# Decoder kernel on one core: couplings on ScalarE, a shorter choice of the expert, first norm in place, queries one turn earlier

## The chip, the core and the metric

The kernel runs on one core of a Trainium2 chip. The core has five engines that run their own instruction streams and meet only at semaphores: TensorE (PE), VectorE (DVE), ScalarE (ACT), GpSimd (POOL) and SyncE (SP), which issues the DMAs. The metric is the device time of one launch in microseconds; smaller is better.

## What is computed

Two decoder layers over x (32 sequences of 256 rows, 256 wide) and a context (32 sequences of 120 rows), with a layer norm behind each of six sublayers:

```python
x = _layernorm(x + _L0_attn_ref(x))          # random features: exp(x P - |x|^2/2) times a fixed matrix
x = _layernorm(x + _L0_xattn_ref(x, ctx))    # cross attention, 16 heads of 16
x = _layernorm(x + _L0_ffn_ref(x))           # 3 cycles of a coupling network, below
x = _layernorm(x + _L1_attn_ref(x))          # Mamba: convolution, gates, scan over 512 channels x 16 states
x = _layernorm(x + _L1_xattn_ref(x, ctx))    # gated unit whose weights are the context
x = _layernorm(x + _L1_ffn_ref(x))           # 8 experts, the one with the highest probability counts
```

The third sublayer computes, three times over, four small layers with gelu and a sigmoid (the "gate"), mixes them with a global gate of the sequence into a coupling, and rotates the state with it: `out = out + coupling * _twist(out)`. The sixth takes `gate = max(softmax(logits))` and `idx = argmax(softmax(logits))` of each row.

## The kernel before

Two sequences (512 rows) make a group, and there are 16 groups. The work on a group is cut into three parts: **f** (sublayers 1 to 3), **m** (the Mamba) and **b** (sublayers 4 to 6 behind the Mamba). A **turn** does f of one group, m of the group before, b of the one before that, and the first steps of the group to come (**nxt**): its random features, keys, values, first projection and first norm. There are 18 turns; f, m and nxt meet in 14 of them (turns 1 to 14, counted from 0), the last two have no f.

Nothing schedules this: on each engine the function `turn` or `turn_` writes the order out by hand, and semaphores tie the engines together. What matters here, with the lines of the program printed below:

- On DVE the spine is `states`, 64 scans (L1087, one for each of 4 channel blocks and 16 states) with 4 output steps (L1093) between, and everything else is put between two of them. A scan reads a decay that ACT has computed into a ring of 12 (`decays`, L1479), and a PSUM bank with the square of the convolved input of its channel block (L1474). ACT computes that square inside `decays`, ahead of decay number `SQUARE_AT[c]`, and not before the last scan of the block in front. The first scan of the last block is number 48; its square stands ahead of decay 59. POOL adds the scanned states up (L1671).
- `norm_add`, `norm_stats` on DVE, `norm_rstd` on ACT (Ln and Exp, L398 and L400), `norm_apply` on DVE (L405), `norm_turn` on PE (8 transposes, L413) and `norm_copy` on ACT (L419) make one layer norm. n1 to n6 are the six norms; `ln1_sum` and `ln3_sum` are the sums and statistics of n1 and n3.
- `cycle` on PE and ACT is one of the three cycles, for both sequences in turn; ACT ends it with the gate (L1430), and `rotate` on DVE computes the coupling (L1038) and the rotation (L1040 to L1043).
- `route` and `pick_expert` on DVE choose the expert, `combine` (L1199) adds the experts' outputs by `experts` on PE (through two banks).
- `mamba_out` on PE brings the residual and the Mamba's output together, in the banks that `experts` used before; it waits for the last `combine`. `rotate_back` transposes the rotated state for `ln3_sum`.
- At a turn's start PE turns n1 and n3, then `mamba_in` (8 products j of 4 matmuls), `queries` (8 matmuls) and `scores` alternate. `scores(f, s, s+1)` makes two products, number u = 2s and u+1, in banks 0, 1 and 2 by turns; for u of 2 and more PE waits until DVE has reduced u-1 of them (`maxima`, L991). DVE's order there is `ln4_sum`, `ln4_apply`, `convolve(m, 0)` (L1064, L1066; it needs j = 0 and 1), `maxima` of the first four products, `convolve(m, 2)` (it needs j = 2 and 3), `maxima` of the others, and then the first scan.

A matmul here is a float32 one of two passes, so one call shows as 2 (two for `queries` make 4 in the order and 8 in the trace).

## Time and profile before

| | us |
|---|---|
| median of 3 runs | 3096.45 (3095.3 to 3101.43) |
| the profiled execution | 3099.29 |
| its span, first to last instruction | 3097.5 |
| one turn in the middle of it | 180.5 |

Some 1.8 us of the profiled execution lie outside its span, and it is 2.8 us above the median. The times in the rows below are microseconds from the span's start. "[2.44 <-ACT gate L1430]" behind a row means that the engine had been idle for 2.44 us, and which instruction ended that. "x4" is the number of instructions that the row merges.

### The profile page before, as it was taken

The page shows a single profiled execution, that of the slowest core. Times are in us where ns is not written, and L with a number is a line of the kernel's source. Part 1 is how long each engine was busy: PE and PEld are TensorE (multiplying, and loading weights), DVE is VectorE, ACT ScalarE, POOL GpSimd, SP SyncE. Part 2 cuts the span into 40 slices and gives each one's busy share as a digit, 9 for nine tenths or more (in the row PEclk, how much of TensorE's full clock was granted, in tenths as well). Part 3 has the DMA queues.
Part 4 walks back from the last instruction along what each step waited for, and adds up shares of the span by engine and source line. Part 5 has one row for each costly group of instructions (what it writes and reads, how often), then busy time and mean ns, then how long its engine had stood idle before and what let it go on. Part 6 is the DMA issues. An engine that isn't in the chain of part 4 may idle for free.

```text
span 3097.5 us, 41602 instructions
## 1 busy us (share of the span) xinstructions
PE 2540.1 (82%) x11020; PEld 1469.9 (47%) x11020; DVE 2495.3 (81%) x4288; ACT 1727.8 (56%) x3062; POOL 1487.4 (48%) x1159
## 2 busy tenths in 40 slices
PE   6896888979888897888988788888888889887556
PEld 3544554544444454445545444554544445454323
DVE  2368888897978889898888978788897888978783
ACT  1457564646657474665646466564656646465620
POOL 1046354554535455563545545354553545456460
PEclk7868888888989989999898899898898989978687
DMA  3000000000000000000000000000000000000000
GB/s 131 10 8 10 14 11 14 17 14 7 10 21 10 14 17 14 7 10 21 10 14 13 18 7 10 21 10 14 13 3 21 10 14 7 7 7 1 14 7 7
DMA packets 16849, 45.72 MB, mean 15 GB/s; under 512 B 2248, under 2 KB 7056, under 8 KB 16400
## 3 DMA queue, kind: packets, MB, share of 16 engines
q1 hardware_dynamic: 16656, 43.96, 4.2%
q14 instruction: 171, 1.40, 0.2%
q8 instruction: 22, 0.36, 0.1%
HBM read 35.57 MB, written 8.39 MB: 14 GB/s over the span
## 4 chain that ended last, share of the span: by engine, by line
PE 47%; DVE 28%; issue 14%; ACT 7%; DVEq 2%; POOL 1%; ACTq 0%; DMA 0%; SPq 0%; POOLq 0%
PE bank L535 45%; DVE h_ring L1087 14%; DVE x L1199 3%; DVE ln_stats L387 2%; DVE smax L991 1%; POOL ysum L1671 1%; ACT a_ring L1479 1%; DVE x L405 1%; DVE xpad L1093 1%; PE bank L413 1%; DVE soft L1066 1%; ACT L1485 1%; ACT L1339 1%; DVE ln_mv L391 1%; ACT spare L1420 1%
## 5 line engine op out<-in xcount | busy, mean ns | idle before, releaser
L1671 POOL TENSOR_TENSOR ysum<-ysum,h_ring 128x512 f32<-128x512 f32 x896 | 1155.2, 1289 | 633.3 <-DVE h_ring L1087 571.3
L1087 DVE TENSOR_TENSOR_SCAN h_ring<-a_ring,bank 128x512 f32<-128x512 f32 x1024 | 1172.7, 1200 | 27.2 <-ACT bank L1474 16.2
L1479 ACT ACTIVATE a_ring<-soft,decay 128x510 f32<-128x510 f32 x1024 | 675.7, 717 | 198.4 <-DVE h_ring L1087 198.0
L535 PE MATMUL bank<-w_expert_w,x45T 128*128 128x512 f32 x1024 | 541.1, 675 | 199.0 <-DVE x L1199 191.4
L535 PEld LDWEIGHTS bank<-w_expert_w,x45T 128*128 128x128 f32 x1024 | 213.2, 216 | 490.9 <-DVE x L1199 253.5
L1658 POOL TENSOR_TENSOR soft<-xc,soft 128x512 f32<-128x512 f32 x64 | 81.0, 1276 | 655.2 <-ACT soft L1457 655.2
L535 PE MATMUL bank<-x3T,w_winT 128*128 128x512 f32 x512 | 291.0, 704 | 39.7 <-ACT x3T L419 31.4
L991 DVE TENSOR_REDUCE smax<-bank 128x4 f32<-128x480 f32 x256 | 156.4, 652 | 143.1 <-PE bank L535 143.1
L535 PE MATMUL bank<-qT,kmask 32*120 32x256 f32 x1024 | 207.2, 497 | 50.2 <-ACT spare L1386 40.6
L535 PE MATMUL bank<-spare,w_cn_w 128*128 128x256 f32 x768 | 217.7, 408 | 37.0 <-ACT spare L1416 22.4
L1199 DVE SCALAR_TENSOR_TENSOR x<-bank,weight,x 128x256 f32<-128x256 f32 x512 | 212.5, 474 | 40.4 <-PE bank L535 40.4
L398 ACT ACTIVATE ln_logv<-ln_mv,eps 128x4 f32<-128x4 f32 x96 | 28.3, 295 | 330.5 <-DVE ln_mv L391 252.7
L535 PE MATMUL bank<-kmask,qT 32*128 32x240 f32 x1024 | 151.8, 417 | 46.1 <-DVE smax L991 45.2
L1386 ACT ACTIVATE spare<-bank 120x512 f32<-120x512 f32 x256 | 138.4, 593 | 81.5 <-PE bank L535 81.4
L535 PEld LDWEIGHTS bank<-x3T,w_winT 128*128 128x128 f32 x512 | 104.3, 220 | 165.1 <-issue 111.5
L535 PEld LDWEIGHTS bank<-spare,w_cn_w 128*128 128x128 f32 x768 | 131.8, 193 | 105.7 <-ACT spare L1416 37.3
L535 PE MATMUL bank<-x12T,w_cn_w 128*128 128x256 f32 x768 | 180.0, 384 | 2.3 <-ACT x12T L1372 2.3
L1671 POOL TENSOR_TENSOR ysum<-h_ring 128x512 f32<-128x512 f32 x64 | 81.3, 1270 | 197.5 <-DVE h_ring L1087 197.5
L413 PE MATMUL bank<-w_ident,x 128*128 128x128 f32 x640 | 127.4, 322 | 49.6 <-DVE x L405 45.6
L535 PEld LDWEIGHTS bank<-x12T,w_cn_w 128*128 128x128 f32 x768 | 146.0, 192 | 40.3 <-issue 20.1
L1416 ACT ACTIVATE spare<-bank,w_columns 128x256 f32<-128x256 f32 x192 | 80.5, 472 | 139.6 <-PE bank L535 139.3
L535 PEld LDWEIGHTS bank<-kmask,qT 32*128 32x128 f32 x1024 | 94.9, 198 | 129.5 <-DVE smax L991 83.8
(149 smaller groups left out, 3890.2 us busy)
## 6 DMA issues: line engine op xcount, KB each, us to landing
x0T<-in_xT SPq DMA_DIRECT2D x16, 512.0 KB, 3.3
x<-in_x SPq DMA_DIRECT2D x16, 512.0 KB, 4.3
out<-x SPq DMA_DIRECT2D x16, 512.0 KB, 3.0
ctxT<-in_ctxT SPq DMA_DIRECT2D x16, 240.0 KB, 2.5
ctxTb<-in_ctxT SPq DMA_DIRECT2D x16, 240.0 KB, 2.7
ctxb<-in_ctx SPq DMA_DIRECT2D x16, 240.0 KB, 3.0
w_expert_w<-in_expert_w SPq DMA_DIRECT2D x1, 2048.0 KB
w_winT<-in_winT SPq DMA_DIRECT2D x1, 1024.0 KB
```

What stands on the lines that cost most here:

```text
L387: n.chain.then(v.bn_stats(n.stats[:, t, :], n.sum[:, t, :]))
L391: last = v.bn_aggr(n.mv[:, t, :], n.stats[:, t, :])
L413: last = pe.transpose(banks[c][:, t * P:(t + 1) * P], n.x[:, t, c * P:(c + 1) * P], ident[:, :])
L535: return pe.matmul(o, l, r, start=start, stop=stop)
L991: v.tensor_reduce(smax[:, t, :].rearrange("p (e r h) -> p r e h", e=DC, r=4)[:, r, :, :], bank[u % 3][:, 0:480].rearrange("p (e h k) -> p ...
L1087: scanned.then(v.tensor_tensor_scan(h_ring[:, k % HRING, :], a_ring[:, k % RING, :, :].rearrange("p b s -> p (b s)"), xc2, 0.0, ALU.mult, ...
L1199: v.scalar_tensor_tensor(out=acc[:, t, :], in0=MB[s % 2][:, e * D:(e + 1) * D], scalar=weight[:, t, x:x + 1], in1=acc[:, t, :], op0=ALU.mu ...
L1386: a.activation(probs[:, s % 4, :, :].rearrange("p k s -> p (k s)"), bank[s % 3][0:KEYS, :], ACT.Exp, scale=1.0 / np.sqrt(DK)).then_inc(pro ...
L1416: a.activation(h1[:, b, r, :], bank[b][:, r * S:(r + 1) * S], ACT.Gelu, bias=col("cn_b1", r)).then_inc(l1_ready.sem, 1)
L1479: a.activation(a_ring[:, k % RING, :, 1:S], delta[:, c, :].rearrange("p (b s) -> p b s", b=NB)[:, :, 1:S], ACT.Exp, scale=decay[:, k:k + 1 ...
L1658: p.tensor_tensor(out=delta[:, c, :], in0=xc[:, c, :], in1=soft[:, c, :], op=ALU.add)\
L1671: p.tensor_tensor(out=total, in0=first, in1=h_ring[:, k % HRING, :], op=ALU.add)\
```

## The change

- The coupling is computed on ACT right behind the gate, and DVE's `rotate` starts from it. So is the global base (L1026).
- The choice of the expert compares the logits with their maximum (they are 0 there after the subtraction) instead of the probabilities, its first part stands ahead of two scans, and the weight is 1 over the sum, since the highest exponential is 1.
- n1 is computed in place over the loaded x0, and its transpose goes into `feats`. DVE does `ln1_sum` two scans earlier and applies n1 two scans behind it, no longer at the turn's end; ACT's `norm_rstd` for it stands ahead of decay 58.
- PE turns n1 between two experts and computes the queries of the next turn behind the last cycle, ahead of `mamba_out`. At the turn's start the first `scores` stand ahead of `mamba_in`, and the second behind its third product. `rotate_back(f, 0)` goes between the second and third part of `mamba_out`.
- The square of block 2 stands ahead of decay 36 instead of 38, and the first rotations behind 33 steps of the scan instead of 32.
- x0 is loaded anew only when POOL has added the bias into x12 and PE has turned n1; POOL's squares in `feats` wait for the queries.

```diff
-SQUARE_AT = (0, 18, 38, 59)
+SQUARE_AT = (0, 18, 36, 59)
...
-        n1, n2, n3 = Norm("ln1", x12, x12T, x0), Norm("ln2", x12, x12T), Norm("ln3", x3, x3T, sum3)
+        n1, n2, n3 = Norm("ln1", x0, feats), Norm("ln2", x12, x12T), Norm("ln3", x3, x3T, sum3)
...
-        QUERY = [bank[2], bank[0]]
-        TURN1 = [bank[0], bank[1]]
+        QUERY = [bank[1], bank[0]]
+        TURN1 = OUT1
...
-                sp.wait_ge(n1.x_ready.sem, n1.x_ready.at(g, NT))
+                sp.wait_ge(x1b_ready.sem, x1b_ready.at(g, 1))
+                sp.sem_inc(held.sem, 1)
+                sp.wait_ge(n1.turned.sem, n1.turned.at(g, DC))
                 sp.sem_inc(held.sem, 1)
...
-            def queries(g):
+            def queries(g, f):
+                if f is not None:
+                    pe.wait_ge(gate_ready.sem, gate_ready.at(f, CYC))
                 pe.wait_ge(n1.xT_ready.sem, n1.xT_ready.at(g, DC))
                 for e in range(DC):
...
                     rotate_back(m, 1)
                 if b is not None:
                     mamba_out(b, IC - 1, IC)
-                if f is not None:
-                    norm_turn(pe, n1, f, TURN1)
                 if m is not None:
                     norm_turn(pe, n3, m, TURN)
-                    mamba_in(m, b, 0, 2)
-                if f is not None:
-                    queries(f)
-                if m is not None:
-                    mamba_in(m, b, 2, 3)
                 if f is not None:
                     scores(f, 0, 1)
                 if m is not None:
+                    mamba_in(m, b, 0, 3)
+                if f is not None:
+                    scores(f, 1, 2)
+                if m is not None:
                     mamba_in(m, b, 3, 4)
-                if f is not None:
-                    scores(f, 1, 2)
                 if b is not None:
...
                 if b is not None:
-                    experts(b, 12, 16)
+                    experts(b, 12, 14)
+                if nxt is not None:
+                    norm_turn(pe, n1, nxt, TURN1)
+                if b is not None:
+                    experts(b, 14, 16)
                 if f is not None:
                     cycle(f, 2 * NB)
-                if m is not None:
-                    mamba_out(m, 0, IC - 1)
+                if nxt is not None:
+                    queries(nxt, f)
+                if m is not None:
+                    mamba_out(m, 0, 2)
                 if f is not None:
                     rotate_back(f, 0)
+                if m is not None:
+                    mamba_out(m, 2, IC - 1)
...
             def rotate(g, s):
...
                 if s == 0:
-                    v.wait_ge(base_ready.sem, base_ready.at(g, 1))
-                v.wait_ge(gate_ready.sem, gate_ready.at(g, s + 1))
-                cyc_chain.link(v.tensor_scalar(couple[:, b, :], gate[:, b, :], gate_scale[:, :], base[:, b:b + 1],
-                                               ALU.mult, ALU.add))
+                    cyc_chain.start(v, g)
+                v.wait_ge(couple_ready.sem, couple_ready.at(g, s + 1))
                 cyc_chain.then(v.tensor_tensor(out=turn[:, 0, b, :], in0=couple[:, b, :], in1=z1, op=ALU.mult))
                 cyc_chain.link(v.tensor_tensor(out=turn[:, 1, b, :], in0=couple[:, b, :], in1=z0, op=ALU.mult))
                 v.tensor_tensor(out=z0, in0=z0, in1=turn[:, 0, b, :], op=ALU.add).then_inc(z_ready.sem, 1)
...
                 v.tensor_tensor(out=logit[:, :, :], in0=logit[:, :, :], in1=over_experts(lmax[:, :]),
                                 op=ALU.subtract).then_inc(logit_ready.sem, 1)
-
-            def pick_expert(g):
+                v.wait_ge(logit_ready.sem, logit_ready.at(g, 1))
+                pick_chain.start(v, g)
+                pick_chain.link(v.scalar_tensor_tensor(out=prank[:, :, :], in0=logit[:, :, :], scalar=0.0,
+                                                       in1=over_tiles(row("rank")), op0=ALU.is_equal, op1=ALU.mult))
+                pick_chain.link(v.tensor_reduce(rmax[:, :], prank[:, :, :], AX, ALU.max))
+                pick_chain.then(v.tensor_tensor(out=pick[:, :, :], in0=prank[:, :, :], in1=over_experts(rmax[:, :]),
+                                                op=ALU.is_equal))
+
+            def weigh_expert(g):
+
                 v.wait_ge(prob_ready.sem, prob_ready.at(g, 1))
-                pick_chain.start(v, g)
-                pick_chain.then(v.tensor_reduce(pmax[:, :], prob[:, :, :], AX, ALU.max))
                 pick_chain.link(v.tensor_reduce(psm[:, :], prob[:, :, :], AX, ALU.add))
-                pick_chain.then(v.reciprocal(pinv[:, :], psm[:, :]))
-                pick_chain.link(v.tensor_tensor(out=pick[:, :, :], in0=prob[:, :, :], in1=over_experts(pmax[:, :]),
-                                                op=ALU.is_equal))
-                pick_chain.then(v.tensor_tensor(out=pgate[:, :], in0=pmax[:, :], in1=pinv[:, :], op=ALU.mult))
-                pick_chain.link(v.tensor_tensor(out=prank[:, :, :], in0=pick[:, :, :], in1=over_tiles(row("rank")),
-                                                op=ALU.mult))
-                pick_chain.link(v.tensor_reduce(rmax[:, :], prank[:, :, :], AX, ALU.max))
-                pick_chain.link(v.tensor_tensor(out=pick[:, :, :], in0=prank[:, :, :], in1=over_experts(rmax[:, :]),
-                                                op=ALU.is_equal))
+                pick_chain.link(v.reciprocal(pinv[:, :], psm[:, :]))
                 pick_chain.end()
-                v.tensor_tensor(out=weight[:, :, :], in0=pick[:, :, :], in1=over_experts(pgate[:, :]),
+                v.tensor_tensor(out=weight[:, :, :], in0=pick[:, :, :], in1=over_experts(pinv[:, :]),
                                 op=ALU.mult).then_inc(weight_ready.sem, 1)
...
                 if b is not None:
-                    pick_expert(b)
+                    weigh_expert(b)
...
-                states(m, 32)
-                if f is not None:
-                    global_base(f)
+                states(m, 33)
+                if f is not None:
                     rotate(f, 0)
                     rotate(f, 1)
                 states(m, 34)
                 states(m, 50)
                 if b is not None:
                     combine(b, 10, 12)
+                if nxt is not None:
+                    ln1_sum(nxt)
                 states(m, 52)
                 if nxt is not None:
-                    ln1_sum(nxt)
-                states(m, 54)
+                    norm_apply(v, n1, nxt)
                 if b is not None:
                     combine(b, 12, 14)
...
                 if f is not None:
                     ln3_sum(f)
-                if nxt is not None:
-                    norm_apply(v, n1, nxt)
                 if f is not None:
...
-            def queries(g):
+            def queries(g, f):
+                if f is not None:
+                    a.wait_ge(z_ready.sem, z_ready.at(f, 2 * CYC))
                 for e in range(DC):
                     a.wait_ge(q_psum.sem, q_psum.at(g, e + 1))
...
+                    a.wait_ge(glob_ready.sem, glob_ready.at(g, 3))
+                    a.activation(base[:, :], gt[:, :], ACT.Identity, bias=base_sign[:, :], scale=glob_scale[:, :])\
+                        .then_inc(base_ready.sem, 1)
...
+                    if s == 0:
+                        a.wait_ge(base_ready.sem, base_ready.at(g, 1))
+                    a.wait_ge(gate_ready.sem, gate_ready.at(g, s + 1))
+                    a.activation(couple[:, b, :], gate[:, b, :], ACT.Identity, bias=base[:, b:b + 1],
+                                 scale=gate_scale[:, :]).then_inc(couple_ready.sem, 1)
...
                 if m is not None:
                     norm_copy(a, n3, m, TURN)
                 if b is not None:
                     norm_rstd(a, n4, b)
                 if m is not None:
-                    mamba_in(m, 0, 2)
-                if f is not None:
-                    queries(f)
-                if m is not None:
-                    mamba_in(m, 2, IC)
+                    mamba_in(m, 0, IC)
                 if b is not None:
...
                 if f is not None:
                     cycle(f, NB)
                     nat()
+                decays(m, 58)
+                if nxt is not None:
+                    norm_rstd(a, n1, nxt)
                 decays(m, STEPS)
+                if nxt is not None:
+                    norm_copy(a, n1, nxt, TURN1)
                 if f is not None:
                     cycle(f, 2 * NB)
                     nat()
+                if b is not None:
+                    norm_rstd(a, n6, b)
                 if nxt is not None:
-                    norm_rstd(a, n1, nxt)
+                    queries(nxt, f)
                 if f is not None:
                     norm_rstd(a, n3, f)
-                if b is not None:
-                    norm_rstd(a, n6, b)
...
                     p.wait_ge(n1.sub_ready.sem, n1.sub_ready.at(g, 0))
+                    p.wait_ge(q_psum.sem, q_psum.at(g, 0))
...
-            def add_bias(g):
-                p.wait_ge(n1.turned.sem, n1.turned.at(g, DC))
+            def add_bias(g, m):
+                p.wait_ge(n1.x_ready.sem, n1.x_ready.at(g, NT))
+                if m is not None:
+                    p.wait_ge(n3.sum_ready.sem, n3.sum_ready.at(m, 2))
                 p.tensor_tensor(out=x1b[:, :, :], in0=n1.x[:, :, :], in1=row("bo").unsqueeze(1).to_broadcast([P, NT, D]),
```

ACT in the loop, late in the turn, where the decays (`a_ring`), the square (`bank<-xc`) and the norm's Ln and Exp stand. Before:

```order
L1479 ACTIVATE a_ring<-soft,decay 128x2x255 [waits scanned]
L1473 ISA
L1474 ACTIVATE bank<-xc 128x512 [waits scanned]
L1477 ISA
L1479 ACTIVATE a_ring<-soft,decay 128x2x255 [waits scanned]
...
L1339 ACT_TABLE_LOAD
L397 REGISTER_ALU
L398 ACTIVATE ln_logv<-ln_mv,eps 128x4 [waits ln1_var_ready]
L399 REGISTER_ALU
L400 ACTIVATE ln_rstd<-ln_logv 128x4 [waits ln1_log_ready]
```

and now:

```order
L1485 ACTIVATE a_ring<-soft,decay 128x2x255 [waits scanned]
L396 REGISTER_ALU
L397 ACTIVATE ln_logv<-ln_mv,eps 128x4 [waits ln1_var_ready]
L398 REGISTER_ALU
L399 ACTIVATE ln_rstd<-ln_logv 128x4 [waits ln1_log_ready]
L1483 ISA
L1485 ACTIVATE a_ring<-soft,decay 128x2x255 [waits scanned]
L1479 ISA
L1480 ACTIVATE bank<-xc 128x512 [waits scanned]
```

Ln and Exp of n1 were behind the last cycle; they now stand two rows of work ahead of the square, with their wait for the statistics (ln1_var_ready).

DVE at the same place, from `combine(10, 12)` to the next scans (`h_ring`). Before:

```order
L1085 ISA [waits xc2_ready]
L1086 ISA [waits summed]
L1087 SCALAR_TENSOR_TENSOR h_ring<-a_ring,bank 128x512 [waits decay_ready]
L1085 ISA
L1086 ISA [waits summed]
L1087 SCALAR_TENSOR_TENSOR h_ring<-a_ring,bank 128x512 [waits decay_ready]
...
L380 TENSOR_TENSOR x<-bank,x 128x512 [waits ln1_sub_ready]
...
L391 BN_AGGR ln_mv<-ln_stats 128x2 x3
L1085 ISA
L1086 ISA [waits summed]
L1087 SCALAR_TENSOR_TENSOR h_ring<-a_ring,bank 128x512 [waits decay_ready]
```

and now:

```order
L379 TENSOR_TENSOR x<-bank,x 128x512 [waits ln1_sub_ready]
...
L390 BN_AGGR ln_mv<-ln_stats 128x2 [waits ln1_chain]
L390 BN_AGGR ln_mv<-ln_stats 128x2 x3
L1081 ISA
L1085 ISA [waits xc2_ready]
L1086 ISA [waits summed]
L1087 SCALAR_TENSOR_TENSOR h_ring<-a_ring,bank 128x512 [waits decay_ready]
L1085 ISA
L1086 ISA [waits summed]
L1087 SCALAR_TENSOR_TENSOR h_ring<-a_ring,bank 128x512 [waits decay_ready]
L402 REGISTER_ALU
L404 TENSOR_SCALAR x<-x,ln_mv,ln_rstd 128x256 [waits ln1_rstd_ready]
```

The sum of n1 (L380, now L379) went ahead of the two scans of which the first waits for the square (xc2_ready), and the application (L404) came behind them.

PE at the start of the loop, from the last transpose of n3: `scores` is kmask,qT, `mamba_in` x3T,w_winT, `queries` x12T,w_wq. Before:

```order
L413 MATMUL bank<-w_ident,x 128x128 [waits ln3_x_ready]
L728 ISA
L535 MATMUL bank<-x3T,w_winT 128x512 [waits ln3_xT_ready]
L535 MATMUL bank<-x3T,w_winT 128x512 x3
L596 ISA
L535 MATMUL bank<-x12T,w_wq 128x512 [waits ln1_xT_ready]
L535 MATMUL bank<-x12T,w_wq 128x512 x3
L734 ISA
L535 MATMUL bank<-x3T,w_winT 128x512 [waits in_read]
L535 MATMUL bank<-x3T,w_winT 128x512
L604 ISA
L605 ISA [waits vals_ready]
```

and now:

```order
L412 MATMUL bank<-w_ident,x 128x128 [waits ln3_x_ready]
...
L609 ISA [waits qT_ready]
L536 MATMUL bank<-kmask,qT 128x240 [waits kmask_ready]
L536 MATMUL bank<-kmask,qT 128x240 x3
L731 ISA
L536 MATMUL bank<-x3T,w_winT 128x512 [waits ln3_xT_ready]
L536 MATMUL bank<-x3T,w_winT 128x512 x3
...
L613 ISA [waits kmask_ready]
L536 MATMUL bank<-kmask,qT 128x240 [waits smax_ready]
L536 MATMUL bank<-kmask,qT 128x240 x3
L737 ISA
L536 MATMUL bank<-x3T,w_winT 128x512 [waits in_read]
```

The queries are gone from here, a first group of scores fills the place ahead of `mamba_in`, and the second (waits smax_ready) stands ahead of the fourth product of `mamba_in` and no longer behind it.

## Rows read from the trace of the kernel before

**Rows 1.** Page, part 1: busy us (share of the span) xinstructions of each engine.

```profile
PE 2540.1 (82%) x11020; PEld 1469.9 (47%) x11020; DVE 2495.3 (81%) x4288; ACT 1727.8 (56%) x3062; POOL 1487.4 (48%) x1159
```

**Rows 2.** Windows: stretch, length, busy of PE, PEld, DVE, ACT, POOL, PEclk, DMA.

```profile
1234.70:1415.20 180.50, 150.20 (x689) 88.18 (x688) 155.58 (x266) 107.44 (x191) 92.78 (x72) 0.92 0.04 13
1595.50:1779.30 183.80, 155.89 (x689) 90.98 (x688) 155.04 (x265) 107.38 (x191) 92.78 (x72) 0.88 0.04 12
```

**Rows 3.** Timeline (start, us, engine, line, op, count, idle before), end of combine(10,12).

```profile
1371.36 1.64 DVE L1199 SCALAR_TENSOR_TENSOR x<-bank,weight,x 128x256 f32<-128x256 f32 x4
1371.47 0.60 ACT L1474 ACTIVATE bank<-xc 128x512 f32<-128x512 f32 x1 [0.39 <-DVE h_ring L1087]
1375.14 1.27 DVE L380 TENSOR_TENSOR x<-bank,x 128x512 f32<-128x512 f32 x2
1377.87 0.38 DVE L391 BATCH_NORM_AGGREGATE ln_mv<-ln_stats 128x2 f32<-128x6 f32 x4
```

**Rows 4.** Timeline: a norm applied on VectorE while GpSimd adds states.

```profile
1283.44 2.62 POOL L1671 TENSOR_TENSOR ysum<-ysum,h_ring 128x512 f32<-128x512 f32 x2 [5.61 <-DVE h_ring L1087]
1284.30 2.56 DVE L405 TENSOR_SCALAR x<-x,ln_mv,ln_rstd 128x256 f32<-128x256 f32 x4
```

**Rows 5.** Timeline: last gate and combine, the residual, rotate_back, third norm, in one turn.

```profile
1395.71 0.48 ACT L1430 ACTIVATE gate<-bank,half_b 128x256 f32<-128x256 f32 x1 [0.35 <-PE bank L535]
1395.97 1.64 DVE L1199 SCALAR_TENSOR_TENSOR x<-bank,weight,x 128x256 f32<-128x256 f32 x4
1397.73 1.98 PE L535 MATMUL bank<-x,w_ident 128*128 128x512 f32 x4 [2.14 <-DVE x L1199]
1404.73 1.04 PE L719 MATMUL bank<-w_ident,x12T 128*128 128x128 f32 x8
1408.11 0.38 DVE L391 BATCH_NORM_AGGREGATE ln_mv<-ln_stats 128x2 f32<-128x6 f32 x4
1409.67 1.39 DVE L405 TENSOR_SCALAR x<-spare,ln_mv,ln_rstd 128x256 f32<-128x256 f32 x4
```

**Rows 6.** Timeline: first matmuls and convolutions of the next turn.

```profile
1414.73 3.70 PE L535 MATMUL bank<-x3T,w_winT 128*128 128x512 f32 x8 [1.95 <-ACT x3T L419]
1419.09 0.88 DVE L1064 TENSOR_SCALAR soft<-xpad,w_columns 128x512 f32<-128x512 f32 x2 [1.97 <-ACT xpad L1437]
1424.62 1.22 DVE L991 TENSOR_REDUCE smax<-bank 128x4 f32<-128x480 f32 x2 [0.67 <-PE bank L535]
1434.15 1.08 PE L535 MATMUL bank<-kmask,qT 32*128 32x240 f32 x8 [0.97 <-DVE smax L991]
```

**Rows 7.** Timeline, PE: eight expert matmuls behind an idle stretch, at two places.

```profile
1364.42 5.40 PE L535 MATMUL bank<-w_expert_w,x45T 128*128 128x512 f32 x8 [4.21 <-DVE x L1199]
1381.71 5.84 PE L535 MATMUL bank<-w_expert_w,x45T 128*128 128x512 f32 x8 [5.00 <-DVE x L1199]
```

**Rows 8.** Timeline: the choice of the expert.

```profile
1297.44 1.25 DVE L1162 TENSOR_TENSOR pick<-prob,pmax 128x32 f32<-128x32 f32 x1
1300.10 1.27 POOL L1676 TENSOR_TENSOR ysum<-ysum,res 128x512 f32<-128x512 f32 x1
1301.97 5.66 DVE L1087 TENSOR_TENSOR_SCAN h_ring<-a_ring,bank 128x512 f32<-128x512 f32 x5 [0.32 <-ACT a_ring L1479]
```

**Rows 9.** Timeline: end of the first cycle.

```profile
1335.34 0.41 DVE L1038 TENSOR_SCALAR couple<-gate,gate_scale,base 128x256 f32<-128x256 f32 x1 [2.44 <-ACT gate L1430]
1335.66 0.47 ACT L1430 ACTIVATE gate<-bank,half_b 128x256 f32<-128x256 f32 x1 [0.36 <-PE bank L535]
1340.44 0.60 ACT L1474 ACTIVATE bank<-xc 128x512 f32<-128x512 f32 x1
1341.26 1.22 DVE L1087 TENSOR_TENSOR_SCAN h_ring<-a_ring,bank 128x512 f32<-128x512 f32 x1 [0.88 <-ACT bank L1474]
```

**Rows 10.** Timeline, DVE: the two rotations of the second cycle.

```profile
1358.74 1.40 DVE L1040 TENSOR_TENSOR qT<-couple,x12T 128x256 f32<-128x256 f32 x1
1361.63 0.43 DVE L1040 TENSOR_TENSOR qT<-couple,x12T 128x256 f32<-128x256 f32 x1
```

More of the change, by code:

```diff
@@ L926, in _ @@
             first_project(0)
+            norm_turn(pe, n1, 0, TURN1)
+            queries(0, None)
             turn(0, None, None, 1)
@@ L1022, in ln2_sum @@
                 norm_stats(v, n2, g)
-            def global_base(g):
-                v.wait_ge(glob_ready.sem, glob_ready.at(g, 3))
-                v.tensor_scalar(base[:, :], gt[:, :], glob_scale[:, :], base_sign[:, :], ALU.mult, ALU.add)\
-                    .then_inc(base_ready.sem, 1)
-                cyc_chain.start(v, g)
             def rotate(g, s):
@@ L1613, in _ @@
             norm_rstd(a, n1, 0)
+            norm_copy(a, n1, 0, TURN1)
+            queries(0, None)
             turn_(0, None, None, 1)
@@ L1681, in turn_ @@
                 if f is not None:
-                    add_bias(f)
+                    add_bias(f, m)
                 if nxt is not None:
```

10 lines of the change are left out of this document (4 added, 6 removed).

## The prediction, on record before the changed kernel ran

> **What bounds the kernel now.** I read the busy shares first: PE 82% and DVE 81% of the span [rows 1], so neither alone is the bound, and the question is who waits at which place of a turn. The windows of whole turns come next: 180.5 us, with DVE busy for 155.6 and PE's granted clock at 0.92; another turn takes 183.8 us with DVE no busier and a clock of 0.88 [rows 2], so some microseconds of a turn go with the clock. Then the timeline of one turn. It has two halves. From the first scan to the last combine DVE goes from one instruction to the next with few waits: what is taken from DVE there is gained, and a wait put on DVE there is lost. From the last combine over the turn's end to the first scan, PE, ACT and DVE wait for each other in one chain, and only its links count.
>
> All sums are for one turn of the kind that has f, m and nxt, in that timeline, and then for the 14 of them, against the profiled execution of 3099.3 us, which is 2.8 above the median.
>
> **A, a new wait of DVE: +2.0 us.** Before, scans 48 and 49 follow combine(10,12) (from 1371.36, 1.64 us) at once; the square for 48 was made on ACT from 1371.47, beside the combine. The sum of n1 starts at 1375.14 and its statistics end at 1378.25, 3.1 us later [rows 3]. Now DVE goes from the combine to the sum, and the statistics end at 1373.0 + 3.1 = 1376.1. ACT has come to Ln of n1 some time before (after decay 57) and waits there; behind it stand Exp, decay 58 and the square of block 3, which scan 48 needs. Ln and Exp take 0.5, the decay 0.6, the square 0.6, and the scan began 0.8 behind the start of another square [rows 9]. That makes 1376.1 + 0.5 + 0.6 + 0.8 = 1378.0, when DVE would have been ready at 1376.0. Nothing else stands on DVE between. Bounds: 1.7 to 2.7, the latter where PE's projection is late, since its 2.2 us of slack are used up too.
>
> **B, n1 is applied in the dense half: +2.5 us.** Four instructions of this kind took 1.39 us at the turn's end [rows 5], when POOL was idle. Behind scans 48 and 49 POOL has just been given a state to add. In the one place where a norm is applied beside POOL's additions, the four took 2.56 us and the second of them stood until POOL's addition was over [rows 4]. Bounds 1.3 and 2.6; I take 2.5, since the neighbourhood is that of rows 4.
>
> The Trainium skill (SBUF — State Buffer, Who interferes with whom) has one port pair between VectorE and GpSimd, held for a whole instruction; in SBUF a tensor_scalar in a two-port mode, and anything with two SBUF inputs, blocks on it. By it the apply pays 1.2 us at the new place, as rows 4 show; without it B would be 1.3 and the whole time about 17 us lower, which is rival 2.
>
> **C, end and start of the turn: +0.6 us.** The last combine ends at 1397.6, call it T [rows 5]. The queries (8 matmuls like the 3.7 us of rows 6) go where PE idled for 2.1 us. They wait for the last gate, which ended at T - 1.4 [rows 5]; with ACT's coupling of the first sequence ahead of it that is T - 1.3, and the residual, which started at T + 0.1, would start at T + 2.4. The last gate may come earlier: the experts(14, 16) ahead of this cycle took 5.84 us behind an idle stretch [rows 7], and now n1's transposes stand ahead of them. If that brings the full clock back they take the 3.7 of rows 6, and the residual starts at T + 0.2. I take the middle, T + 1.3, so 1.2 later than before. Behind it stands the same PE work as before (residual, three parts of mamba_out, both rotate_back, done at T + 8.2 [rows 5]), now done at T + 9.4; the third norm's second half waits for that, so that two couplings less on DVE bring nothing. What was hidden under the application of n1, ACT's Ln and Exp of n3, becomes a wait of 0.6 behind the statistics, but the application itself (1.3) is gone: n3 is ready at T + 13.9 in place of T + 13.4 [rows 5]. Behind it stand eight transposes and one copy less, and scores fill the gap ahead of mamba_in, which for that starts 0.8 to 1.3 us sooner behind n3: at T + 16.3 to 16.8 in place of T + 17.1, and so convolve(0), which follows it by 4.4 [rows 6].
> Here the moved scores give it back. Product 2 waits for the first reduction, and DVE makes that only behind convolve(0). PE is done with three products of mamba_in 5.5 behind its first (each 1.85, being half of 3.7); the reduction comes at convolve(0)'s start + 5.5 [rows 6], which is 9.9 behind it: PE stands for 4.4 us. Then come two scores (1.1) and the fourth product (1.8), then ACT's copy (0.6), and only then convolve(2) (4.9). After an idle stretch of 4.2 us eight matmuls took 5.40 us [rows 7] in place of 3.70 [rows 6], so I add 1.7. The pair of products 6 and 7, before at T + 36.5 [rows 6], comes at convolve(0)'s start + 5.5 + 1.1 + 1.8 + 1.7 + 0.6 + 4.9 + 0.6 = + 16.2. With convolve(0) at T + 20.7 to 21.2 that is T + 36.9 to 37.4, a loss of 0.4 to 0.9. Bounds: with the residual at T + 0.2 and full clock behind the idle stretch a gain of 2.2, and with the residual at T + 2.4 a loss of 2.
>
> **D, choice of the expert: -0.45.** From pick (1297.44) on, each instruction with two SBUF inputs ended where one of POOL's additions ended [rows 8]. One such comparison, a maximum and a product go. But the weight, which was made while POOL was idle, now falls behind the two scans, when POOL works at the last states and the scaling (1.27) [rows 8]. By POOL's cadence the weight would end at 1301.2 and the scan start at 1301.5, against 1301.97. Bounds: 0.2 and 1.6 gained.
>
> **E, first cycle: -0.6.** DVE waits 2.44 for the gate, then 0.88 for the square of block 2 [rows 9]. One scan more fills the first wait. The square then decides: it moves ahead of two decays (1.3), and behind two couplings of ACT, which cost 0.64 (the second gate starts 0.14 later, then 0.5 for its coupling, by the gate's 0.47) [rows 9]. So the square starts 0.6 earlier, at 1339.8, and the scan at 1340.7. Bounds 0 and 1.4.
>
> **F, second cycle: -0.45.** There the first product took 1.40 us, until POOL was done, and that of the second sequence 0.43 [rows 10]; I expect the first to end when it did with or without a coupling ahead; the second coupling (0.41 as in rows 9, and a gap) goes. **The third cycle** lies under C's PE chain: 0.
>
> The added waits on SP (x0 loaded later) and POOL (the squares in feats behind the queries) I cost at nothing: the x0 now loaded at the turn's end is wanted by n1's sum late in the next turn, and POOL, busy for 92.8 of 180.5 us [rows 2], has slack for the squares; if x0 came too late, A's wait would be longer by what is missing.
>
> **The sum.** +2.0 + 2.5 + 0.6 - 0.45 - 0.6 - 0.45 = +3.6 a turn. Against it I set 0.4 for residual and mamba_out, which no longer follow an idle stretch of PE and so will more often find the full clock (3.3 us separate the turns of rows 2; an estimate). +3.2 by 14 turns is +45. The turn with f but no nxt has neither A nor B: -2.5. The last two gain 0.3 each by D; the first, without m, nothing. Together +42: 3141 for the profiled execution, 3138 for the median.
>
> **Rivals.**
> 1. **Better clock (faster).** n1's transposes and the queries fill two of PE's gaps, so that experts(14, 16) take 3.7, the queries end with the combine, and PE doesn't fall to the low clock in C's idle stretch. C is then -2.2, the sum +0.4 a turn, and with half of the 3.3 us by which the turns of rows 2 differ -1.2: 3099 - 17 - 3 - 3 = 3076 for the median. It decides where the stretches below 0.9 of the granted clock get fewer. For it: the 3.3 us of rows 2. Against it: 4.2 us of idle cost 1.7 [rows 7], and A and B stay.
> 2. **B without the lock.** DVE's four instructions go through ahead of POOL's addition: 1.2 by 14 less, 3121. Against it rows 4.
> 3. **A wash.** Only the first part of that clock: C's residual at T + 0.2 (-1.2), and D and E at their upper bounds (1.1 and 0.8 more): 3.1 by 14 less, 3095.
> 4. **Much slower.** If the queries run at half clock (7.4 us) they end 3.7 later, and so does the residual with all behind it: +3.7 by 14 turns, 3190 were it so in each; in one turn of three 3155.
>
> **How the numbers follow.** Chances: forecast 0.42, B without the lock 0.12, a wash 0.13, faster 0.18, much slower 0.15. The range goes from 3082 to 3158: it leaves out most of the faster rival and the extreme of the slower one. A measurement tells 0.2% (6 us) from no change. Slower holds forecast, rivals 2 and 4, 0.69; same the wash, 0.13; faster rival 1, 0.18.
>
> **What would show it.** A: DVE idle for about 2 us ahead of the scan behind ln1's statistics, released by ACT's square. B: the four instructions of n1 at 2.5 us. C: the residual over 1 us behind the last combine, PE idle for over 4 us ahead of the second scores. D: the choice of the expert shorter by under 1 us. E: the first rotation's wait for the gate near 1.2, and a wait for the square of block 2 left. I would be wrong if the square didn't hold scan 48, if the residual followed the last combine as now, or if the stretch from T to the products 6 and 7 shrank from 36.5 us to under 35.

## The result and the profile of the changed kernel

The changed kernel takes 3145.25 us (median, 3144.16 to 3146.16), the kernel before 3095.88 beside it: a ratio of 1.0153 with a 95% interval of 1.0135 to 1.0171. It is slower by 49 us. Page of the changed kernel, the span and the busy time of each engine, to be read against [rows 1]:

```profile
span 3144.4 us, 41641 instructions
## 1 busy us (share of the span) xinstructions
PE 2588.9 (82%) x11020; PEld 1480.0 (47%) x11020; DVE 2451.8 (78%) x4128; ACT 1778.9 (57%) x3174; POOL 1490.4 (47%) x1159
```

DVE has 44 us less to do than in [rows 1] and 90 us more idle time; PE, with the same 11,020 matmuls, is busy for 49 us more, at a granted clock of 0.859 in place of 0.872. In the windows view one turn of the changed kernel reads so (columns as in [rows 2]):

```profile
1435.87:1620.17 184.30, 158.12 (x688) 90.68 (x688) 152.90 (x257) 110.73 (x198) 93.07 (x73) 0.88 0.04 13
```

Every turn of the changed kernel takes 184.3 us; those of before ranged from 177.9 to 186.1, with 181.95 in the mean. **Turns 3 to 14, cut into stages at marks on DVE** (starts taken from the timeline, T is the start of the statistics behind the last combine, and each number is a mean over the 12 turns, in us):

| stage | before | after | square_first | scores_back | small_parts | pe_filler |
|---|---|---|---|---|---|---|
| T to convolve(0) | 23.07 | 20.83 | 22.06 | 20.82 | 23.00 | 19.20 |
| convolve(0) to convolve(2) | 9.59 | 11.79 | 11.81 | 7.73 | 9.60 | 7.73 |
| to the first scan | 18.69 | 18.14 | 18.14 | 18.28 | 18.53 | 18.51 |
| to the logits | 26.51 | 26.61 | 24.29 | 24.57 | 26.18 | 25.21 |
| to the weight's end | 7.45 | 4.96 | 4.85 | 5.14 | 5.44 | 5.34 |
| to combine(0, 2) | 20.54 | 21.88 | 21.85 | 21.69 | 20.91 | 21.27 |
| to combine(4, 6) | 20.86 | 20.44 | 20.44 | 20.43 | 20.43 | 20.44 |
| to combine(10, 12) | 28.96 | 28.70 | 28.69 | 28.70 | 28.70 | 28.70 |
| to combine(12, 14) | 9.05 | 11.04 | 9.15 | 11.03 | 9.05 | 9.16 |
| to the next T | 17.23 | 19.93 | 19.93 | 19.93 | 17.23 | 19.93 |
| turn | 181.95 | 184.33 | 181.21 | 178.33 | 179.05 | 175.48 |

The 47 us between the two profiled spans lie in three places: T of the first turn of the loop comes at 514.2 in place of 490.9 (+23), 12 turns add 2.4 each (+28.5), and the end is 5 shorter.

Where A and B were expected, on DVE of the changed kernel (timeline, columns as in [rows 3], which they answer):

```profile
1404.90 1.64 DVE L1197 SCALAR_TENSOR_TENSOR x<-bank,weight,x 128x256 f32<-128x256 f32 x4
1406.46 1.28 DVE L379 TENSOR_TENSOR x<-bank,x 128x512 f32<-128x512 f32 x2
...
1409.19 0.38 DVE L390 BATCH_NORM_AGGREGATE ln_mv<-ln_stats 128x2 f32<-128x6 f32 x4
1411.46 2.33 DVE L1087 TENSOR_TENSOR_SCAN h_ring<-a_ring,bank 128x512 f32<-128x512 f32 x2 [1.89 <-ACT bank L1480]
1413.71 2.31 DVE L404 TENSOR_SCALAR x<-x,ln_mv,ln_rstd 128x256 f32<-128x256 f32 x4
1415.94 1.65 DVE L1197 SCALAR_TENSOR_TENSOR x<-bank,weight,x 128x256 f32<-128x256 f32 x4
1417.51 3.43 DVE L1087 TENSOR_TENSOR_SCAN h_ring<-a_ring,bank 128x512 f32<-128x512 f32 x3
1420.86 1.19 DVE L1093 SCALAR_TENSOR_TENSOR xpad<-ysum,w_columns,xc 128x512 f32<-128x512 f32 x1
```

Scan 48 waits 1.89 us for ACT's square, and the four applications take 2.31, not 1.4. The last row is the output step, 0.73 before and 1.19 here, a cost that is not in the forecast. Between the combine at 1415.94 and the last one stand 14 scans where 12 stood: scans 50 and 51 moved behind it. On PE, the same turn's end and the next one's start (timeline; to be read against [rows 5] and [rows 6]):

```profile
1431.16 3.69 PE L536 MATMUL bank<-feats,w_wq 128*128 128x512 f32 x8 [0.88 <-ACT gate L1431]
1435.97 1.98 PE L536 MATMUL bank<-x,w_ident 128*128 128x512 f32 x4 [1.11 <-DVE x L1197]
...
1447.64 1.74 PE L412 MATMUL bank<-w_ident,x 128*128 128x128 f32 x8 [1.91 <-DVE x L404]
1449.39 1.08 PE L536 MATMUL bank<-kmask,qT 32*128 32x240 f32 x8
1450.65 7.07 PE L536 MATMUL bank<-x3T,w_winT 128*128 128x512 f32 x12 [0.18 <-ACT x3T L418]
1462.14 1.97 PE L536 MATMUL bank<-kmask,qT 32*128 32x240 f32 x8 [4.42 <-DVE smax L999]
1464.04 3.77 PE L536 MATMUL bank<-x3T,w_winT 128*128 128x512 f32 x4
```

The queries are over 1.0 us ahead of the last combine's end and delay nothing; the residual follows it at once. mamba_in starts at T + 14.8, 2.3 earlier than in the turn of [rows 6], but its 12 matmuls take 7.07 us where 8 took 3.70 [rows 6] (at that rate 12 take 5.55). Then PE stands for 4.42 us, and behind that the scores take 1.97 and not 1.08, and the fourth product 3.77, twice the 1.85 of [rows 6].

### The profile page after: what moved, and what is told of

It reads as the page before. It is cut to its first block, busy times and chain, and to the rows that moved or that the text cites. A ratio compares the mean times of both kernels' runs of the same rounds, so it can differ in the third digit from the quotient of the medians.

```text
span 3144.4 us, 41641 instructions
## 1 busy us (share of the span) xinstructions
PE 2588.9 (82%) x11020; PEld 1480.0 (47%) x11020; DVE 2451.8 (78%) x4128; ACT 1778.9 (57%) x3174; POOL 1490.4 (47%) x1159
## 4 chain that ended last, share of the span: by engine, by line
PE 50%; DVE 24%; issue 14%; ACT 9%; DVEq 2%; POOL 0%; ACTq 0%; DMA 0%; SPq 0%; POOLq 0%
PE bank L536 49%; DVE h_ring L1087 10%; DVE x L1197 3%; DVE x L404 2%; DVE ln_stats L386 2%; DVE soft L1066 2%; DVE smax L999 1%; PE bank L412 1%; ACT a_ring L1485 1%; ACT L1335 1%; ACT gate L1431 1%; ACT L1491 1%; ACT xpad L1443 1%; DVE ln_mv L390 1%; ACT bank L1480 1%
## 5 line engine op out<-in xcount | busy, mean ns | idle before, releaser
L536 PE MATMUL bank<-w_expert_w,x45T 128*128 128x512 f32 x1024 | 521.1, 654 | 126.3 <-DVE x L1197 119.9
L536 PEld LDWEIGHTS bank<-w_expert_w,x45T 128*128 128x128 f32 x1024 | 204.5, 207 | 397.3 <-issue 210.9
L536 PE MATMUL bank<-x3T,w_winT 128*128 128x512 f32 x512 | 323.3, 778 | 12.3 <-ACT res L1446 8.3
L536 PE MATMUL bank<-qT,kmask 32*120 32x256 f32 x1024 | 216.3, 516 | 48.4 <-ACT spare L1384 40.2
L412 PE MATMUL bank<-w_ident,x 128*128 128x128 f32 x640 | 136.7, 330 | 141.3 <-DVE x L404 137.4
L536 PE MATMUL bank<-kmask,qT 32*128 32x240 f32 x1024 | 160.4, 436 | 107.4 <-DVE smax L999 106.5
L536 PE MATMUL bank<-spare,w_cn_w 128*128 128x256 f32 x768 | 215.4, 404 | 23.1 <-ACT spare L1417 8.6
L412 PEld LDWEIGHTS bank<-w_ident,x 128*128 128x128 f32 x640 | 89.4, 158 | 223.5 <-DVE x L404 183.7
L536 PEld LDWEIGHTS bank<-x3T,w_winT 128*128 128x128 f32 x512 | 113.8, 239 | 155.1 <-issue 132.3
```

Source lines behind the costliest of these rows:

```text
L412: last = pe.transpose(banks[c][:, t * P:(t + 1) * P], n.x[:, t, c * P:(c + 1) * P], ident[:, :])
L536: return pe.matmul(o, l, r, start=start, stop=stop)
```

## The experiments

The names are those of the table. Each time is a median; the kernel before was timed beside each at 3098 to 3101, spread from 3078 to 3114, on three chips in all. All comparisons with the changed kernel are with its 3145.

**square_first.** On ACT:

```diff
-                decays(m, 58)
+                decays(m, 60)
                 if nxt is not None:
                     norm_rstd(a, n1, nxt)
```

> The changed kernel with one edit: on ScalarE the Ln and Exp of n1 stand behind the square of block 3 and decay 59 (two decays later), no longer ahead of them. Theory (term A is a wait of its own): the 1.89 us that DVE stands ahead of scan 48 go in each of 14 turns and nothing comes late behind them, since the norm is applied only two scans (2.3 us) later: 27 us less than the changed kernel's 3145, so 3118. Rival (the next wait takes over): ACT comes to Ln late, DVE then waits ahead of the application, or the turn's end is bound by PE and ACT anyway; then less than a third comes back and the time is 3136 or more.

3105.09 us, 40 less than the changed kernel; against before 1.0024 (1.0006 to 1.0041). The stage to combine(12, 14) shrinks by 1.89 us, and DVE doesn't wait there:

```profile
1568.46 0.38 DVE L390 BATCH_NORM_AGGREGATE ln_mv<-ln_stats 128x2 f32<-128x6 f32 x4
1568.85 2.33 DVE L1087 TENSOR_TENSOR_SCAN h_ring<-a_ring,bank 128x512 f32<-128x512 f32 x2
```

So A is shown, at its size. The other 13 us come from elsewhere: the stage to the logits is 2.3 shorter and the one to convolve(0) 1.2 longer, with nothing in them edited. The stage to the logits goes with the clock in most of these kernels: here it takes 23.9 us in 10 of 12 turns, at a granted clock of 0.90, and 26.4 and 26.6 in the two others, at 0.82; in the changed kernel it takes 26.6 in every turn, at 0.82. Scores_back has turns of both kinds too. The kernel before has none as short: 24.9 us in two turns, at 0.91, and 26.4 to 27.0 in the others, at 0.75 to 0.82. The mean clock isn't all of it (square_and_scores has turns of 25.1 us at 0.75), and why an edit elsewhere changes this stage isn't shown.

**scores_back.** On PE:

```diff
-                if f is not None:
-                    scores(f, 1, 2)
                 if m is not None:
                     mamba_in(m, b, 3, 4)
+                if f is not None:
+                    scores(f, 1, 2)
```

> The changed kernel with one edit: on TensorE scores 2 and 3 stand behind the fourth product of mamba_in and no longer ahead of it; scores 0 and 1 stay ahead of mamba_in. Theory (term C's hollow): PE's idle stretch of 4.42 us ahead of the fourth product goes, convolve(2) starts 9.6 us behind convolve(0) as in the kernel before and not 11.8, and 2.2 us a turn come back: 30 us in 14 turns, 3115. Rival (given back behind it): the six pairs of maxima and the scores behind them are bound by PE at half clock whatever stands ahead, the first scan moves by under 0.5 us a turn, and the time is 3138 or more.

3069.84, 75 less than the changed kernel (0.9907 of before, 0.9878 to 0.9937). PE in the same place:

```profile
1418.94 8.79 PE L536 MATMUL bank<-x3T,w_winT 128*128 128x512 f32 x16 [0.22 <-ACT x3T L418]
1430.43 1.08 PE L536 MATMUL bank<-kmask,qT 32*128 32x240 f32 x8 [2.70 <-DVE smax L999]
```

The idle stretch ahead of the fourth product is gone, and convolve(2) follows convolve(0) by 7.73, which is DVE's own work: 1.86 less than even before, since the first scores are ready when convolve(0) ends. C's hollow (PE's idle stretch ahead of the fourth product) cost 4.06 us a turn against this order and not 2.2, and 2.0 more come from the stage to the logits. Two turns of this kernel, that stage in the windows view (columns as in [rows 2]), show its two values with the clock of each:

```profile
1450.81:1474.69 23.88, 20.48 (x184) 12.94 (x188) 22.79 (x32) 19.19 (x34) 14.59 (x12) 0.90 0.07 21
1806.57:1833.18 26.61, 22.90 (x186) 13.80 (x188) 22.91 (x32) 19.43 (x34) 14.59 (x12) 0.82 0.06 19
```

This edit alone turns the loss into a gain; square_first alone comes within 0.24% of the kernel before.

**square_and_scores**, both edits.

> The changed kernel with both edits of the two runs ahead of it. They lie in different halves of a turn with DVE dense between, so if each theory holds the gains add: 3145 - 27 - 30 = 3088. If the two are bound by one chain, this is no faster than the better of the two.

3064.17. The two local gains (1.89 and 4.06 us a turn) are both there, but the sum isn't: T to convolve(0) is 22.0 and the stage to the logits 25.3. PE at the turn's start:

```profile
1411.62 2.25 PE L412 MATMUL bank<-w_ident,x 128*128 128x128 f32 x8 [1.91 <-DVE x L404]
1413.80 1.97 PE L536 MATMUL bank<-kmask,qT 32*128 32x240 f32 x8
1415.70 9.01 PE L536 MATMUL bank<-x3T,w_winT 128*128 128x512 f32 x16
```

The scores ahead of mamba_in now take 1.97 us too (1.08 in the changed kernel). The granted clock from T to convolve(0) is 0.84 to 0.85, and 0.92 in scores_back: what is gained on DVE is partly taken back by PE at the low clock.

**small_parts.** The kernel before with the couplings, the expert's choice, the square at 36 and the rotations at 33 (their lines of the diff above), without n1, queries and scores.

> The kernel before with the small parts alone: couplings and base on ScalarE, the shorter choice of the expert, square of block 2 ahead of decay 36, first rotations behind 33 scans. n1, the queries, the scores and mamba_out stay where they were. Theory (D, E and F as the two traces show them, 0.5, 0.4 and 0.3 us a turn): 1.2 us less in 14 turns, 17 us, so 3079 against 3096; n1 and the queries then cost the changed kernel 66 us. Rival (each is waited away before the turn's end, the waits for attention and for the gate take them up): within 5 us of the kernel before.

3055.77 (0.9852, 0.9814 to 0.989), 45 less than before: far more than the 17 expected of these parts. By the table the turn is 2.9 us shorter, 2.0 of it in the stage to the weight's end; in the profiled runs another 10 us go behind the last turn of the table, where nothing was looked into. The six times spread from 3038 to 3067. So n1, queries and scores in the new order cost the changed kernel 89 us: between the two profiled spans, 5.3 a turn in the 12 turns, 22 up to the first T of the loop and 5 at the end.

**expert_only.** Of the diff the shorter choice of the expert alone.

> The kernel before with one part of the change alone: the shorter choice of the expert. In the changed kernel the stretch from the logits to the weight is 2.5 us shorter, but the stretch from there to the first combine 1.3 us longer. Theory (DVE only moves its wait to the attention): net 1.1 us in each of 15 turns, so 17 us less than before. Rival (the gain is kept, the 1.3 us belongs to another part of the change): 2.4 us a turn, 35 us less. By the forecast's own term D it would be 0.45 a turn, 7 us.

3075.5 (0.9933, 0.9908 to 0.9958): 25 less than before. Logits to weight take 5.06 where they took 7.45, and the stage behind, 20.42, gives nothing back. So the theory that the stage behind takes 1.3 us of it back is refuted here; that longer stage of the changed kernel comes with the other parts. But the time, 25 us less, lies between theory (17) and rival (35), and in the profiled run the turn is only 1.0 us shorter (180.96): T to convolve(0) takes 24.3 there in place of 23.1, at a granted clock of 0.74 to 0.79 in 7 of 12 turns (4 in the kernel before). In the trace of this kernel two of the small instructions still stand until POOL's addition is over:

```profile
1295.51 1.30 DVE L1155 SCALAR_TENSOR_TENSOR prank<-logit,w_rows 128x32 f32<-128x32 f32 x1
1296.85 0.19 DVE L1157 TENSOR_REDUCE rmax<-prank 128x4 f32<-128x32 f32 x1
1297.07 0.97 DVE L1158 TENSOR_TENSOR pick<-prank,rmax 128x32 f32<-128x32 f32 x1
...
1300.61 0.19 DVE L1167 TENSOR_TENSOR weight<-pick,pinv 128x32 f32<-128x32 f32 x1
```

**apply_behind.** To square_and_scores, on DVE (and on PE n1's transposes behind experts(14, 16)):

```diff
-                if nxt is not None:
-                    norm_apply(v, n1, nxt)
                 if b is not None:
                     combine(b, 12, 14)
+                if nxt is not None:
+                    norm_apply(v, n1, nxt)
```

> The kernel of square_and_scores with the application of n1 behind combine(12, 14) and no longer ahead of it, on TensorE its transposes behind experts(14, 16). GpSimd has then caught up during the 1.6 us of the combine. Theory (B is a lock between the two engines): the four instructions take 1.4 us and not 2.3, 0.9 us in 14 turns, 13 us less than square_and_scores (3064): 3051. Rival (B is the price of four instructions wherever they stand, or what is saved is lost to GpSimd's addition a scan later): within 4 us of 3064.

3071.44. B's size beside POOL is shown: in the changed kernel POOL adds from 1413.87 to 1415.22, just after the first of the four has started at 1413.71; here POOL's addition has ended at 1560.61, and the same four instructions behind the combine take 1.38 us,

```profile
1560.73 1.38 DVE L404 TENSOR_SCALAR x<-x,ln_mv,ln_rstd 128x256 f32<-128x256 f32 x4
```

and from combine(10, 12) to T the turn is 0.93 us shorter. But the time rises by 7: the stages from T to the logits add 1.5 us a turn (74.8 in place of 73.3).

**pe_filler.** To square_and_scores, on PE ahead of n3's transposes, two products that nobody uses (the edit of this run against square_and_scores):

```diff
+                if m is not None and f is not None:
+                    pe.wait_ge(qT_ready.sem, qT_ready.at(f, DC))
+                    for k in range(2):
+                        mm(bank[k][:, :], wq[:, 0, 0:P], n1.xT[:, 0, :], True, True)
                 if m is not None:
                     norm_turn(pe, n3, m, TURN)
```

> The kernel of square_and_scores with two more matmuls of 512 columns (4 passes) on TensorE ahead of n3's transposes, once the queries are copied; their result is overwritten by the scores and used by nobody. They fill the 1.9 us for which TensorE stands there. Theory (with the queries gone from the turn's start mamba_in runs at half clock because nothing keeps TensorE busy ahead of it): its first two products take 3.7 us in place of 5.5, convolve(0) starts 1 to 1.8 us earlier, 14 to 25 us less: 3040 to 3050. Rival (the granted clock there doesn't depend on this gap, or n3's transposes now come later): 3064 or more.

3027.94 (0.9769, 0.9744 to 0.9795): more work on PE, 36 us less time.

```profile
1391.88 1.88 PE L536 MATMUL bank<-feats,w_wq 128*128 128x512 f32 x4
1393.96 1.74 PE L412 MATMUL bank<-w_ident,x 128*128 128x128 f32 x8 [0.19 <-DVE x L404]
...
1396.98 7.13 PE L536 MATMUL bank<-x3T,w_winT 128*128 128x512 f32 x16 [0.24 <-ACT x3T L418]
1406.82 1.08 PE L536 MATMUL bank<-kmask,qT 32*128 32x240 f32 x8 [2.71 <-DVE smax L1003]
1407.83 1.87 PE L412 MATMUL bank<-w_ident,x 128*128 128x128 f32 x8
1409.50 2.82 PE L536 MATMUL bank<-x3T,w_winT 128*128 128x512 f32 x4
```

The idle 1.9 us ahead of the transposes are filled, the scores take 1.08 us again and the 16 matmuls of mamba_in 7.13 in place of 9.01 (square_and_scores), and T to convolve(0) falls from 22.0 to 19.2, with a granted clock of 1.00 in every turn in place of 0.84 to 0.85. The low clock of mamba_in was the price of PE's gap. The last two rows, n4's transposes and the next product, are slower here than in square_and_scores (1.10 and 1.88 there).

**startup_order.** To square_and_scores, in turns 0 and 1 alone n1's transposes and copies behind the third cycle.

> The kernel of square_and_scores with another order in the first two turns alone, which have no experts: n1's transposes and copies stand behind the third cycle, no longer ahead of it. Theory (the changed kernel loses 16 us up to the first turn of the loop because the third cycle waits there for n1): 7 us less in turn 0 and up to 3 in turn 1, so 3054 to 3057. Rival (the loss sits in the turn's start, as in every turn): within 3 us of 3064.

3073.71, 9.5 more. The third cycle does come earlier in turn 0 (its rotations at 151.8 in place of 154.3, though the first ones are at 126.7 in place of 124.6, which the edit doesn't explain), but the queries behind it now wait 2.96 us for the copies, take 5.37 in place of 3.70 and hold up rotate_back: convolve(0) starts 2.6 later there and 6.6 later in turn 1. Where the 16 us at the start (T at 508.8 in square_and_scores, 492.4 in small_parts) come from stays open; filler_apply, below, has 499.2.

**before_filler, small_filler.** The kernel before, and small_parts, with two such products ahead of n1's transposes (bank 3, constant operands):

> The kernel before with two more matmuls of 512 columns (4 passes) ahead of n1's transposes at the turn's start, their result used by nobody; nothing else is changed. TensorE stands there for 1.35 us. Theory (the half clock at the turn's start is a cost of the kernel before too, in its slower turns): the stretch from the last combine to convolve(0), 23.1 us in the mean and 21.6 at best, comes near its best in every turn: 1.5 us in 14 turns, 20 us less. Rival (only the changed order, with the queries gone, is cold there): within 5 us of before, or 0.5 us a turn more since the transposes now start 0.5 later.

> The kernel of small_parts (3056) with the same two matmuls ahead of n1's transposes. If they help the kernel before by 20 us they help here by as much: 3036. It is then the question whether n1, queries and scores in the new order (pe_filler, 3028) are worth anything at all: by these numbers 8 us.

3112.8 (1.0047, 1.0021 to 1.0073) and 3071.32: 15 us more each. T to convolve(0) is 24.1 and 25.2 in the mean, up from 23.1 and 23.0. A part of that is neither clock nor order. In 2 of 12 turns of before_filler and 3 of 12 of small_filler, PE stands 3.9 to 5.6 us between the transposes of rotate_back, ahead of the filler, and the profile shows nothing that it waits for (PE, before_filler):

```profile
503.54 0.60 PE L719 MATMUL bank<-w_ident,x12T 128*128 128x128 f32 x4
507.24 0.90 PE L719 MATMUL bank<-w_ident,x12T 128*128 128x128 f32 x3 [3.10 <-issue]
510.14 0.47 PE L719 MATMUL bank<-w_ident,x12T 128*128 128x128 f32 x1 [2.00 <-issue]
```

No other run has such a stretch in its 12 turns. It makes 0.85 and 1.2 us a turn in the mean, of the 1.1 and 2.2 by which T to convolve(0) is longer; its cause isn't shown. Behind the filler n1's and n3's transposes do run faster (16 of them in 1.91 to 2.86 us, and in 3.05 to 3.99 without it), yet in the turns without the stall the stage is no shorter than in the same kernel without the filler (23.3 against 23.1 in the mean, 24.4 against 23.0). So these two runs show that such a filler isn't a gain everywhere, but not that its place alone decides.

**filler_apply.** pe_filler with the order of apply_behind.

> The kernel of pe_filler with n1 applied behind combine(12, 14), as in apply_behind. There the 0.9 us of the lock came back, and 1.5 us a turn were lost in stretches at half clock at the turn's start. Theory (that loss was the clock's, and the filler keeps it): 0.9 us in 14 turns, 13 us less than pe_filler's 3028: 3015. Rival (the loss belongs to the later transposes of n1): 3035.

3041.07, 13 more than pe_filler. The time is on the rival's side: T to convolve(0) stays at 19.2, so it isn't the turn's start, but the three stages behind it are each 0.8 us longer. That makes 1.7 us a turn, 21 us in 12 turns; against it the first T of the loop comes 8.4 us earlier (499.2). Why a later n1 does either isn't shown.

**two_fillers.** pe_filler with two more products behind mamba_in's fourth:

> The kernel of pe_filler with two more such matmuls (4 passes) behind the fourth product of mamba_in, ahead of scores 2 and 3, where TensorE stands 2.71 us in pe_filler and then takes 1.87 us for n4's transposes and 2.82 for the next product, both about half as fast as elsewhere. Theory (that stretch is cold because of the idle one ahead, and it is on the path): transposes and product take 1.0 and 1.9, the stretch from convolve(2) to the first scan is 0.5 to 1.5 us shorter, 7 to 21 us less than pe_filler's 3028. Rival (as in before_filler: filling helps one place and the low clock comes at another one later, or the stretch isn't on the path): 3028 or more.

3016.19 (0.9713, 0.9681 to 0.9745), the lowest median of all, 4.1% below the changed kernel; its times (3004 to 3023) overlap a little with those of pe_filler (3020 to 3029). Behind the second pair the transposes and the product run at full clock:

```profile
1408.89 1.09 PE L412 MATMUL bank<-w_ident,x 128*128 128x128 f32 x8
1409.82 1.88 PE L536 MATMUL bank<-x3T,w_winT 128*128 128x512 f32 x4
```

The stages behind it gain little of that (18.24 for 18.51, 24.97 for 25.21): the turn is 0.7 us shorter in the profiled runs, 8 of the 12 us, and the first T comes 4 earlier.

## Why the prediction was right

The time came out at 3145 for a forecast of 3138, on the side that was forecast. Its terms stand less well than the total: that it is so near is luck, as the sum at the end of this section shows.

- **A, right.** +2.0 forecast; the wait is 1.89 us, the stage 1.99 longer, and taking it away gave 1.89.
- **B, right, with a part missed.** +2.5 forecast; 2.31 for the four, and 0.93 of it was POOL's addition (apply_behind). By the Trainium skill's rule on the port pair (SBUF — State Buffer, Who interferes with whom) one engine holds the pair for a whole instruction and the other waits until it ends; here the trace agrees: 2.31 beside POOL's addition, 1.38 without. Missed: the output step, 0.46 longer at its new place. A and B together +4.7 (11.04 + 19.93 against 9.05 + 17.23).
- **C, the hollow right, the step on the residual wrong.** PE stood for 4.42 us (4.4 forecast), the scores and the product behind ran at half clock, and convolve(2) came 2.2 later. But the residual was not 1.2 late: it followed the last combine by 0.1 as before, which the prediction had named as a sign of being wrong. The step that failed: "The last gate may come earlier", by the experts' speed alone. I had not counted that combine(12, 14) now has two more scans (2.3 us) between it and the last combine, so that the gate came at T - 4.8 and the queries were hidden. A part of that gain was lost at mamba_in, whose first products ran at half clock behind a gap of 1.91 us. From T to the first scan the changed kernel takes 50.8 us: 0.6 shorter than the mean before, not 0.6 longer. The rows behind C were of one turn, whose 49.7 us are among the shortest; in the others T to convolve(0) went up to 26.4 at a granted clock of 0.74, and the changed kernel takes 20.8 at 0.92 in each. One turn was too few to forecast from.
- **D, mis-sized.** -0.45 forecast, bounds 0.2 to 1.6. Logits to weight is 2.5 shorter; in this kernel the stage behind is 1.3 longer, in expert_only it isn't. I had expected the instructions that remain to pay one addition of POOL each; most of them fell between two.
- **E and F.** -0.6 and -0.45 forecast, -0.42 and -0.26 measured. E's wait for the gate stayed at 2.3 us where I had expected 1.2: I had counted the wait up to the coupling, but what waits now is the product behind it, 0.5 later, and the base, 0.4, is gone from DVE ahead of it.
- **Clock.** -0.4 forecast; the granted clock fell, from 0.872 to 0.859 over the span. The forecast's first rival rested on the clock, and the experiments bear that out in part: one filled gap gave 36 us, and the edit that took away the gap of 4.42 gave 75, of which 57 are the stage itself (4.06 in 14 turns).
- **The first turns, missed.** I gave turns 0 to 2 some 6 us; they cost 23. In turn 0 n1's norm, in front of the third cycle, has no scans to hide it: the third rotations come at 154.6 in place of 147.3. These 7 us are the part that is explained.

The total is near because these errors cancel: the 12 turns cost 28.5 where the forecast had 3.2 each, 38; the start cost 17 more; the end gained 5 where I had 3. The mechanisms A and B and the hollow of C, 6.9 us a turn together, carry the verdict. Either of A and the hollow decides whether the kernel is slower: without A it is level with the kernel before (1.0024), and without the hollow, one placing of four lines on PE, it is faster (0.9907).

## What to carry to other kernels

In these runs a gap on TensorE cost twice, by the time that it stood and by the slower matmuls behind it (9.01 us in place of 7.13): when work is moved out of a place, see what the work behind it will run at, and put no wait that another engine releases late between two pieces of dense matmul. Before a norm's small steps are put on an engine ahead of what the spine needs, write down who waits for what stands behind them. Measure a bundle by its parts: here three small ones gained 45 us and the large one lost 89. And look at all turns before a number is taken from one: the kernel before had turns of 177.9 to 186.1 us with the same instructions.

## What the runs showed of the hardware

- A filler of 4 passes (1.88 us) in a gap of 1.9 us made 16 matmuls of 512 columns take 7.13 us in place of 9.01, and the whole kernel 36 us faster; a like filler ahead of 16 transposes in the kernel before made it 15 us slower; in its profiled run PE stood 5.1 us in each of two turns at a place where it waited for nothing that the profile shows, and the cause is open. I expected neither the size of the first nor the sign of the second.
- Four tensor_scalar instructions of 128x256 take 1.38 us alone and 2.31 to 2.56 beside GpSimd's additions of 1.3; an instruction with two inputs of 128x32 takes 0.19 or, beside one, 0.92 to 1.3.
- One stage of attention, whose instructions no run edited, takes 23.9 us in most turns of square_first and scores_back, at a granted clock of 0.90, and 26.6 in all turns of the changed kernel, at 0.82; with that an edit of 1.9 us a turn was worth 40 us in place of the 27 of 14 turns.
